# A gated state-space block on one core: filler products for PE and a direct silu in the opening

## What is computed

```python
# xattn: 4 sequences of L=512, DI=512 channels, DS=16 states per channel
x = in_proj_w @ hidden                       # 512 x 256 times 256 x 512, per sequence
xc = causal_conv(x, conv_w, 4 taps) + conv_b
u = silu(xc)
x_dbl = x_proj_w @ u                         # 48 rows: dt_lo (16), B (16), C (16)
delta = softplus(dt_proj_w @ dt_lo + dt_proj_b)
for t in range(L):                           # for each channel and each of its 16 states
    state = state * exp(delta[t] * A) + delta[t] * u[t] * B[t]
    y[t] = sum_n state[n] * C[n, t]
y = (y + D * u) * silu(layernorm(x_in))
x2 = x_in + tanh(g_xattn) * y
# ffn: top 2 of 32 experts of rank 16 on layernorm(x2)
out = x2 + tanh(g_ffn) * sum_s gate_s * (h @ U_s) @ V_s * (0.9 + 0.2 * gate @ sigmoid(attr @ Wa))
```

## Time and profile before

| | us |
|---|---|
| median of 3 runs | 548.91 |
| lowest and highest | 548.59, 549.83 |
| the profiled execution's own time | 550.42 |
| its span, first to last instruction | 548.6 |
| first scan starts, from the span's start | 33.40 |

### The profile page before, as it was taken

How to read it: one execution, slowest core, us unless ns; L and a number is a source line. 1 busy time by engine, 2 the same in 40 slices (tenths; PEclk the granted TensorE clock), 3 DMA queues, 4 the chain that set the end, 5 groups by cost and what they waited for, 6 DMA issues and landing times.

```text
span 548.6 us, 9113 instructions
## 1 busy us (share of the span) xinstructions
PE 490.2 (89%) x2962; PEld 361.4 (66%) x2962; DVE 481.8 (88%) x884; ACT 393.8 (72%) x704; POOL 456.5 (83%) x337
## 2 busy tenths in 40 slices
PE   6687989898888799999998999998999999899688
PEld 2156979767766486766776776657666666675654
DVE  3868999978989999979999999889899889999852
...
DMA packets 18705, 39.37 MB, mean 72 GB/s; under 512 B 5585, under 2 KB 6353, under 8 KB 18658
## 3 DMA queue, kind: packets, MB, share of 16 engines
...
## 4 chain that ended last, share of the span: by engine, by line
PE 53%; DVE 21%; ACT 13%; issue 9%; POOL 2%; DMA 1%; DVEq 0%; ACTq 0%; SPq 0%; POOLq 0%
PE p_s L744 12%; PE p_y L766 11%; DVE state L1228 10%; PE p_v L799 7%; PE p_f L790 6%; PE p_tr L711 3%; PE p_pr L667 3%; PE p_pr L674 3%; ACT da L985 2%; PE p_pr L686 2%; DVE x L1170 2%; DVE p_s L1228 2%; PE p_f L779 1%; ACT L938 1%; ACT p_s L985 1%
## 5 line engine op out<-in xcount | busy, mean ns | idle before, releaser
L564 POOL TENSOR_TENSOR state<-state,c_bc 128x1024 f32<-128x1024 f32 (+1 forms) x131 | 256.5, 1970 | 21.7 <-DVE state L1228 19.6
L744 PEld LDWEIGHTS p_s<-pair_b,du_t 128*128 128x128 f32 x1072 | 139.4, 198 | 41.9 <-issue 29.7
L744 PE MATMUL p_s<-pair_b,du_t 128*128 128x128 f32 x1072 | 152.8, 285 | 13.6 <-DVE state L1228 10.6
L549 POOL TENSOR_TENSOR dbu<-du,pair_b 128x1024 f32<-128x1024 f32 (+1 forms) x80 | 145.2, 1818 | 5.6 <-DMA pair_b<-bc_rows 4.2
L766 PE MATMUL p_y<-ident,state 128*128 128x128 f32 x1024 | 148.7, 275 | 0.0
L985 ACT ACTIVATE p_s<-delta,a_neg 128x512 f32<-128x512 f32 (+1 forms) x162 | 93.6, 581 | 66.9 <-DVE state L1246 33.5
L1228 DVE TENSOR_TENSOR_SCAN state<-da,p_s 128x512 f32<-128x512 f32 (+1 forms) x116 | 134.5, 1173 | 7.3 <-PE p_s L744 6.7
L766 PEld LDWEIGHTS p_y<-ident,state 128*128 128x128 f32 x1024 | 120.8, 143 | 23.7 <-issue 22.7
L985 ACT ACTIVATE da<-delta,a_neg 128x512 f32<-128x512 f32 (+1 forms) x158 | 100.4, 648 | 15.6 <-DVE state L1228 15.3
L1228 DVE TENSOR_TENSOR_SCAN state<-p_s,dbu 128x512 f32<-128x512 f32 (+1 forms) x100 | 98.3, 998 | 1.9 <-POOL dbu L549 1.8
L790 PE MATMUL p_f<-u_sb,h_t 128*128 128x512 f32 x112 | 56.9, 612 | 1.2 <-DVE gw L1329 1.2
...
## 6 DMA issues: line engine op xcount, KB each, us to landing
c_bc<-bc_rows SPq DMA_DIRECT2D x32, 512.0 KB, 5.4
pair_b<-bc_rows SPq DMA_DIRECT2D x16, 512.0 KB, 6.2
...
cx<-in_ctx_t SPq DMA_DIRECT2D x4, 512.0 KB, 3.5
...
```

What stands on the lines that cost most here:

```text
L549: eng.tensor_tensor(dbu[:, i % 2, :, 0:w], du[:, 0:w].unsqueeze(1).to_broadcast([P, 2, w]), rows_of_b(p)[:, :, c0:c0 + w], ALU.mult).then_ ...
L564: eng.tensor_tensor(pair, pair, c_bc[:, 2 * p:2 * p + 2, c0:c0 + w], ALU.mult).then_inc(po_cs, 1)
L744: mm = eng.matmul(p_s[g % BANKS][:, t * P:(t + 1) * P], du_t[:, f % 2, t, :], diagonals_of(n // 2)[:, n % 2, c0 // P + t, :], start=(t == ...
```

## The change

Two things are done in the opening, and what hangs on them is moved.

1. **Filler products.** PE makes products of a tile of ones (`ot[:, 0:P]`, set by a memset that now leads POOL's program) with itself into `p_y`, which nobody reads (`keep_clock(count)`, 128x128 each): 9 before `in_projection(0)`, 3, 2, 4 and 6 ahead of the four products of `small_projection(0)`, 3 ahead of `dt_projection(0)`, 6 ahead of `turn_du(0)` and 2 behind it, 35 in all.
2. **u by ACT alone.** For blocks 0 to 3 ACT makes u with its own Silu (`silu_first`) straight from the taps; the halving of `cw` and `cb` moves behind the taps, and `tanh_v` and `silu_u` of these blocks are gone. Block 4 keeps the old way, but its tanh moves from n = 5 to n = 14 and its `silu_u` from n = 6 to n = 15 of phase 0.
3. **Tables.** The loads are placed by hand: Exp at the start, Silu behind the Exp of `a_neg`, and a set that holds both Exp and Ln behind `copy_small(0)`. `copy_b(0)` moves ahead of the softplus.
4. **aw** is made in PSUM (`p_y_rows`), 1 + x at n = 6, the reciprocal at n = 7.
5. **SP** issues the store of the B and C rows and their broadcasts ahead of the loads of x for sequence 1 and of `u_sb`, and pair 2 of B ahead of pair 0 of C.
6. **POOL** builds one diagonal ahead of `scale_of_z(0)`, and three instead of two ahead of its first `times_b`.

```diff
--- before.py
+++ after.py
@@ -150,7 +150,6 @@
         half = sb("half", [P, Q])
-        table = sb("table", [P, 1])
         a_neg = sb("a_neg", [P, Q, NS])
@@ -232,6 +231,7 @@
+        po_one = sem("pool_ones")
         po_k = sem("pool_constants")
@@ -249,6 +249,7 @@
         ac_cv = sem("act_conv_started")
+        ac_u = sem("act_u")
         ac_th = sem("act_tanh_v")
@@ -375,6 +376,13 @@
                 eng.wait_ge(ve_du, 1)
+        def wait_for_u(eng, count):
+            if count <= Q:
+                eng.wait_ge(ac_u, count)
+            else:
+                eng.wait_ge(ve_u, count - Q)
@@ -446,18 +454,18 @@
             load_ctx(1)
+            store_bc(0)
+            broadcast_b(0, 0)
+            broadcast_b(0, 2)
+            broadcast_c(0, 0)
+            broadcast_c(0, 1)
+            broadcast_b(0, 5)
+            broadcast_c(0, 2)
+            for p in range(3, PAIRS):
+                broadcast_c(0, p)
             for k in range(Q):
...
             eng.dma_start(u_sb[:, :, :], u_w.rearrange("(c p) n -> p c n", p=P)).then_inc(s_uv, 16)
-            store_bc(0)
-            broadcast_b(0, 0)
-            broadcast_c(0, 0)
-            broadcast_b(0, 2)
-            broadcast_c(0, 1)
-            broadcast_c(0, 2)
-            broadcast_b(0, 5)
-            for p in range(3, PAIRS):
-                broadcast_c(0, p)
             eng.dma_start(v_sb[:, :, :], v_w.rearrange("(c p) n -> p c n", p=P)).then_inc(s_uv, 16)
@@ -491,6 +499,7 @@
         def _(eng):
+            eng.memset(ot[:, 0:P], 1.0).then_inc(po_one, 1)
             eng.memset(w_small[:, :, DR:BROW], 0.0).then_inc(po_k, 1)
@@ -588,11 +597,12 @@
+            diagonals(0, 1)
             scale_of_z(0)
-            diagonals(0, 1)
             diagonals(0, 2)
+            diagonals(0, 3)
             times_b(0, pool_pairs(0)[0])
-            for i in range(3, len(pe_pairs(0))):
+            for i in range(4, len(pe_pairs(0))):
                 diagonals(0, i)
@@ -670,7 +680,7 @@
                 for k in blocks:
-                    eng.wait_ge(ve_u, Q * b + Q if b else k + 1)
+                    wait_for_u(eng, Q * b + Q if b else k + 1)
                     mm = eng.matmul(p_pr[0:BROW + 2 * NS, :], w_small[:, k, :], u[:, (Q * b + k) % U_RING, :],
@@ -682,7 +692,7 @@
                 if f > 1:
-                    eng.wait_ge(ve_u, min(f + Q, BLOCKS))
+                    wait_for_u(eng, min(f + Q, BLOCKS))
                 eng.matmul(p_pr[:, 0:w], w_dt[:, e * P:(e + 1) * P], xd[0:DR + 1, c0:c0 + w],
@@ -750,7 +760,7 @@
                 else:
-                    eng.wait_ge(ac_k, 4)
+                    eng.wait_ge(ve_k, 6)
                 for t in range(PHASE[f][3] // P):
@@ -809,16 +819,28 @@
+            def keep_clock(count):
+                for i in range(count):
+                    eng.matmul(p_y[:, i % Q, :], ot[:, 0:P], ot[:, 0:P], start=True, stop=True)
+            eng.wait_ge(po_one, 1)
+            keep_clock(9)
             eng.wait_ge(s_first, 16)
...
             eng.wait_ge(po_k, 9)
-            small_projection(0, range(Q))
+            for k, count in enumerate((3, 2, 4, 6)):
+                keep_clock(count)
+                small_projection(0, [k])
+            keep_clock(3)
             dt_projection(0)
...
             in_projection(4)
+            keep_clock(6)
             turn_du(0)
+            keep_clock(2)
             for f in range(F):
@@ -908,6 +930,10 @@
+            def silu_first(q):
+                eng.wait_ge(ve_tap, 3 * q + 3)
+                eng.activation(u[:, q % U_RING, :], conv_v(q), ACT.Silu).then_inc(ac_u, 1)
             def tanh_v(q):
@@ -988,6 +1014,8 @@
                     eng.wait_ge(pe_skip, f)
+                else:
+                    eng.wait_ge(ac_u, Q)
                 eng.activation(skipped[:, 0:w], u[:, (Q * b + k) % U_RING, c0:c0 + w], ACT.Copy,
@@ -1065,24 +1093,28 @@
-            eng.wait_ge(po_k, 6)
-            eng.activation(table[:, :], minus_half[:, 0:1], ACT.Exp)
-            eng.wait_ge(ve_k, 2)
+            eng.preload_act_table(ACT.Exp)
+            eng.wait_ge(s_conv, 32)
             conv_first(0)
-            for q in range(1, Q):
-                conv_first(q)
-                tanh_v(q - 1)
-            tanh_v(Q - 1)
+            conv_first(1)
             eng.wait_ge(s_second, 16 * 6)
             eng.activation(a_neg[:, :, :], a_neg[:, :, :], ACT.Exp).then_inc(ac_k, 1)
+            eng.preload_act_table(ACT.Silu)
+            conv_first(2)
+            silu_first(0)
+            conv_first(3)
+            silu_first(1)
             eng.wait_ge(s_w, 16 * 5)
...
             eng.activation(gf[:, :], gf[:, :], ACT.Tanh).then_inc(ac_k, 1)
+            silu_first(2)
+            silu_first(3)
             eng.wait_ge(po_k, 9)
             copy_small(0)
+            eng.preload_act_table_set("natural_log_exp_and_others")
+            copy_b(0)
             softplus(0, 0)
             softplus(0, 1)
-            copy_b(0)
             softplus(0, 2)
@@ -1097,11 +1129,9 @@
                         conv_first(4)
-                    if f == 0 and n == 5:
-                        tanh_v(4)
                     if f == 0 and n == 4:
                         eng.wait_ge(pe_k, 1)
-                        eng.activation(aw[:, :], p_y_rows[:, 0:S], ACT.Exp, scale=-1.0).then_inc(ac_k, 1)
+                        eng.activation(p_y_rows[:, S:2 * S], p_y_rows[:, 0:S], ACT.Exp, scale=-1.0).then_inc(ac_k, 1)
                     if n == 0 and mid >= 0 and mid % Q == 0:
@@ -1134,6 +1164,8 @@
                         z_part(f, 1)
+                        if f == 0:
+                            tanh_v(4)
                     if n == 15:
@@ -1172,7 +1204,7 @@
             def silu_u(q):
-                eng.wait_ge(ac_th, q + 1)
+                eng.wait_ge(ac_th, q - Q + 1)
                 if q >= U_RING:
@@ -1313,6 +1345,8 @@
                     made(3)
+                    if T == 0:
+                        eng.wait_ge(ve_k, 6)
                     eng.tensor_scalar(a[:, 1:2], z_sum[:, i:i + 1], GATE_EPS, a[:, 0:1], ALU.mult, ALU.add).then_inc(ve_g, 1)
@@ -1339,20 +1373,17 @@
-            eng.wait_ge(s_conv, 32)
-            eng.tensor_scalar(cw[:, :, :], cw[:, :, :], 0.5, None, ALU.mult).then_inc(ve_k, 1)
-            eng.tensor_scalar(cb[:, :], cb[:, :], 0.5, None, ALU.mult).then_inc(ve_k, 1)
-            eng.wait_ge(ve_k, 2)
             def taps(q):
...
-            taps(0)
-            for q in range(1, Q):
+            eng.wait_ge(s_conv, 32)
+            for q in range(Q):
                 taps(q)
-                silu_u(q - 1)
-            silu_u(Q - 1)
+            eng.wait_ge(ve_tap, 3 * Q)
+            eng.tensor_scalar(cw[:, :, :], cw[:, :, :], 0.5, None, ALU.mult).then_inc(ve_k, 1)
+            eng.tensor_scalar(cb[:, :], cb[:, :], 0.5, None, ALU.mult).then_inc(ve_k, 1)
             eng.wait_ge(s_w, 16 * 5)
@@ -1361,6 +1392,7 @@
                 z_statistics(q)
+            eng.wait_ge(ve_k, 4)
             combine(0)
@@ -1374,13 +1406,11 @@
                     if f == 0 and n == 6:
-                        silu_u(4)
+                        eng.wait_ge(ac_k, 4)
+                        eng.tensor_scalar(p_y_rows[:, 2 * S:3 * S], p_y_rows[:, S:2 * S], 1.0, None, ALU.add).then_inc(ve_k, 1)
                     if f == 0 and n == 7:
-                        eng.wait_ge(ac_k, 4)
-                        eng.tensor_scalar(aw[:, :], aw[:, :], 1.0, None, ALU.add).then_inc(ve_k, 1)
                         eng.wait_ge(ve_k, 5)
-                        eng.reciprocal(aw[:, :], aw[:, :]).then_inc(ve_k, 1)
-                        eng.wait_ge(ve_k, 6)
+                        eng.reciprocal(aw[:, :], p_y_rows[:, 2 * S:3 * S]).then_inc(ve_k, 1)
                     if n == (1 if f % Q else 14) and f + Q < BLOCKS:
@@ -1427,6 +1457,8 @@
                             f_statistics(T, 2)
+                    if f == 0 and n == 15:
+                        silu_u(4)
                     if n == 15 and f + 5 < BLOCKS:
```

## The result

| | median us | range | runs |
|---|---|---|---|
| before | 549.23 | 546.12 to 551.06 | 17 |
| changed | 543.69 | 542.27 to 546.74 | 17 |

The ratio is 0.9914 (95% interval 0.9898 to 0.9931), some 5 us less. 538.4 was forecast and 543.5 was the upper end of the range, so the direction was right and the size wrong by half. The profiled execution of the changed kernel took 542.47 with a span of 540.7, that is 7.95 less than the profiled one of before; 10.5 was forecast for that pair.

The account below looks back on a forecast made before the run. Bound: an uncovered opening chain, then DVE with POOL close behind. Terms 8.0 (third scan) + 3.0 (phase 0) + 0.1 - 0.6 = 10.5 off 548.91 gave 538.4 us; own range 537.0 to 539.6, 8 in 10 within 536.6 to 543.5.

Parts of the forecast that it names:

- Step 1: Opening, start to taps: fillers raise PE's clock early, `conv_first(0)` starts at 7.1 instead of 8.79, 1.7 us earlier.
- Step 2: Opening, taps to small products: last u ready at 17.6, `copy_small` at 19.2 instead of 24.30, 5.1 us earlier.
- Step 3: Opening, `copy_small` to first scans: first scan at 26.25 instead of 33.40, third scan 8.0 us earlier.
- the term 8.0: End of the opening: third scan starts at 28.55 instead of 36.58, 8.0 us earlier.
- Step 4: Phase 0 on DVE: a wait, `silu_u(4)` and most of the 2.32 addition leave before the second `combine`, 3.0 us together.
- Step 5: POOL's first `times_b` at 27.3, 7.7 us earlier; DVE waits 1.2 at n = 10; phase 0 ends 10.5 earlier.
- B: Rival: POOL is the bound, margins used up in phases 0 to 2, gain 8.8 to 9.5 us; chance 0.12.
- A: Rival in the opening: fillers do not hold PE's clock, gain 5.6, time 543.3 us; chance 0.13 with milder forms.
- C: Rival: later phases give back a part through new waits or a clock fall, 543 to 546 us; chance 0.07.
- D: Rival in PE's queue: slower, the clock never rises before the small products, 557 us; chance 0.04.
- E: Rival on ACT: Silu or the joint table misbehaves, three more loads on the path, 542.3 us; chance 0.03.

Follow-up runs that it names:

- the repeat: The changed kernel run once more with nothing altered, for a second trace; ratio 0.9908 to the kernel before.

## Why the prediction missed

**Step 1** held in the first trace (`conv_first(0)` 7.14, forecast 7.1) and in the third nearly (8.11), but not in the repeat: ctx landed at 5.77, twelve products took 7.64 instead of 5.39, and `conv_first(0)` came at 9.62, later than the 8.79 of before. By the traces' clock records the rate first rose at 4.87, 10.30 and 7.21 in the changed kernel, and at 8.71, 10.20 and 11.33 in the kernel before. A start that one trace shows isn't a constant.

**Step 2** held to the last silu (17.69, forecast 17.6). The fillers and products ahead of the fourth small product were added up wrongly (12.1 + 15 x 0.24 + 3 x 0.93 is 18.5, not 18.1) and sized too low. A filler took 0.27 (1.60 for six) rather than 0.24, a small product, two records, 1.0 rather than 0.93: 19.06 instead of 18.1.

**Step 3**: the table load stood where it should (Abs 22.34, that 1.0 later), B pair 0 landed 5.4 rather than 5.05 behind `copy_small`, and DVE's two products took 2.19 instead of 1.3 beside POOL's selects. First scan 28.45 instead of 26.25, the third 30.70 without a wait. That collision was not in the sum; in the kernel with the swap alone it was 2.9. In the two other traces of the changed kernel there was none (1.29 and 1.31), but `copy_small` came 2.9 and 1.0 later. So the term 8.0, third scan earlier, measured 5.9 in the first pair and 4.9 on the means of three traces each. By size this is the largest miss of the sum.

**Step 4** held as to DVE (0.17 for the addition; 3.5 for the phase, forecast 3.0), but was counted as gain for the end. It stood on a margin of 1.1 for POOL, read from one trace, and on the wait of 1.18 for the taps of block 5 behind it, which the others don't have; in both others of the kernel before POOL's product ends 0.04 before scan (0, 10), and there 2.3, 0.6 or 0.24 taken off DVE only lengthen a wait.

**Step 5** had the right mechanism, a wait for POOL at n = 10 (1.73, forecast 1.2), and a wrong start: this is the step that failed most for the end. POOL's first `times_b` was forecast 7.7 earlier, at 27.3; it came 5.5 earlier in the first pair and 4.4 on the means. Of the 3.3 that are missing, 2.1 are `copy_small` (5.1 forecast, 3.0 measured). The other 1.2 lie between there and POOL's start (8.6 behind the end of `copy_small`, where the forecast has 7.4). B pair 2 does land about as assumed, 7.7, 7.7 and 7.9 behind the end of `copy_small` in the three traces (7.4 forecast). But POOL itself is later: it gets b_t at 22.5 and then has a select, the scale of z and two more selects in front, to 29.45. The moved diagonal doesn't lie in a gap, as I had it; there is hardly one left.

**Sum.** In the pair of first traces POOL's start, 2.15 later than forecast, makes 10.5 into 8.35; scan (1, 0) shows 8.36, and 0.4 more is lost behind it. The other half of the miss is that the pair isn't typical: the first trace of before is the one in which DVE was late at scan (0, 10). With three traces of each kernel, the means are:

| | before | changed | |
|---|---|---|---|
| `copy_small` ends | 25.2 | 22.2 | 3.0 |
| from there to the first `times_b` starts | 10.1 | 8.6 | 1.5 |
| from there to scan (0, 10) if POOL bounds | 15.8 | 14.8 | 1.0 |

That makes 5.5; the spans' means, 547.6 and 542.3, differ by 5.3, and the medians by 5.5. So the gain is 3.0 of silu and fillers together (without fillers 3.4, in one trace), and 2.5 of the swapped broadcast and the diagonal together. How these 2.5 divide is not shown. With the swap undone 1.3 are lost, so the table's 1.5 and 1.0 are one reading. The other: in the three traces B pair 2 lands at 28.6, 31.5 and 29.8, and POOL comes 0.9, 1.0 and 0.7 later, because one diagonal more (1.06) stands in front; by that the move is worth an estimated 0.1 to 0.3 and the swap the rest. The near agreement of 5.5 and 5.3 is partly luck: at scan (0, 10) the means differ by 5.8, since DVE was late in the first trace of before, and 0.5 is given back in phase 5. Joint table and addition act on DVE's path, which has to keep up; what they save shows in no time here.

**Rivals.** B, POOL is the bound, was right as a mechanism, and wrong in its price (8.8 to 9.5), since it used the same start of POOL. A has nearly the time that came out, 543.3, for a reason that didn't occur: the clock held, to 32 or later in all three traces. C occurred in a small part, in phase 5: two of the three traces of the changed kernel have about what the kernel before has there (29.9 and 29.6 against 29.5 to 29.8), the third 30.7. That its range, 543 to 546, holds the measured time is luck: most of the shortfall arose in the opening. D didn't occur. E didn't: Silu took 0.63, and one load of 1.28 stands where it was meant. No drain shows with a table switch: b_t is copied 0.01 after the load's end. What the Trainium skill (TensorE: Matmul & The Clock Gate, "What's actually happening") says of slow products at a start, that their number varies between runs of one kernel, the traces bear out: 5.39, 6.39 and 7.64 for the same twelve. I had given it 1.1 at most; `copy_small` alone spreads over 2.9 in the three traces.
